# First mixture of a two-layer decoder: other queues for its loads, two scatters under way, one wait for each tile's entry

## The reference

```
x += self_attention(layernorm(x))          # layer 0, 16 heads of 64
x += cross_attention(layernorm(x), ctx)    # layer 0, 16 heads of 16
x += mixture0(layernorm(x))                # layer 0: 8 experts of 704, top 2, and a shared one of 352
x += linear_attention(layernorm(x))        # layer 1
x += cross_attention(layernorm(x), ctx)    # layer 1, 16 heads of 64
x += mixture1(layernorm(x))                # layer 1: 64 experts of 128, top 8, and a shared one
```

## Time and profile before

| | us |
|---|---|
| median of 3 runs | 3784.36 |
| lowest, highest | 3773.11, 3792.74 |
| the profiled execution, whole | 3764.9 |
| its span (first to last instruction) | 3763.2 |
| TensorE busy | 3304.6 (88%) |
| VectorE, ScalarE, GpSimd busy | 1865.9, 1650.9, 846.2 |

### The profile page before, as it was taken

The page is one execution under the profiler, slowest core; times in us unless marked ns, Lnnn a source line. Parts: engine busy times, 40 slices in busy tenths (PEclk is TensorE's granted clock), DMA queues, the critical chain, the costliest instruction groups (busy, mean ns, idle before and its releaser), DMA issues. The chain is left out here.

```text
span 3763.2 us, 76649 instructions
## 1 busy us (share of the span) xinstructions
PE 3304.6 (88%) x24490; PEld 2470.7 (66%) x24491; DVE 1865.9 (50%) x5115; ACT 1650.9 (44%) x4558; POOL 846.2 (22%) x920
## 2 busy tenths in 40 slices
PE   5999996899999777499996988999999999959882
PEld 4777775666666554277774766777777777746762
DVE  3555553677777642022221663556565665642333
ACT  2555553666666410022221325666656565621220
POOL 0000000000000033133332110132323233241774
PEclk9999998999999888799998999999999999979996
DMA  8400003000000231111112000010000000012885
GB/s 275 114 0 0 0 0 135 11 10 8 10 9 10 88 85 48 19 31 30 29 29 55 0 18 27 16 39 19 18 12 12 15 11 13 10 57 90 225 212 138
DMA packets 152369, 181.52 MB, mean 48 GB/s; under 512 B 46428, under 2 KB 126425, under 8 KB 151276
## 3 DMA queue, kind: packets, MB, share of 16 engines
q1 hardware_dynamic: 102476, 137.64, 12.3%
q0 software_dynamic: 47808, 26.74, 4.4%
q10 hardware_dynamic: 2016, 16.25, 1.0%
HBM read 116.17 MB, written 103.88 MB: 58 GB/s over the span
## 5 line engine op out<-in xcount | busy, mean ns | idle before, releaser
L1203 DVE TENSOR_REDUCE e_nmx<-PS 128x1 f32<-128x361 f32 x416 | 221.2, 532 | 400.4 <-PE PS L1044 384.8
L1554 ACT ACTIVATE b_p<-PS,b_nmx 100x361 f32<-100x361 f32 x512 | 275.5, 569 | 162.4 <-DVE b_nmx L1641 162.4
L847 POOL DMA_INDIRECT slot_rows<-r_row,r_rows_now x256 | 255.7, 999 | 401.2 <-DVE e_p L1210 274.8
L1044 PE MATMUL PS<-e_cT,e_qT 128*128 128x361 f32 x832 | 330.1, 479 | 0.0
L1150 ACT ACTIVATE e_pT<-PS 121x384 f32<-121x384 f32 (+1 forms) x416 | 199.2, 479 | 226.2 <-PE PS L1051 219.4
L1641 DVE TENSOR_REDUCE b_nmx<-PS 100x1 f32<-100x361 f32 x512 | 247.5, 526 | 97.6 <-PE PS L1404 95.8
L2509 PE MATMUL PS<-c_wgu,c_tile_xT 128*128 x912 | 290.5, 462 | 1.3 <-ACT c_tile_xT L2564 1.3
L1051 PEld LDWEIGHTS PS<-ident,e_p 128*121 128x121 f32 x1248 | 199.7, 186 | 96.6 <-issue 1.1
L1155 ACT ACTIVATE e_p<-PS,e_nmx 128x361 f32<-128x361 f32 x416 | 232.6, 559 | 69.4 <-DVE e_nmx L1203 67.4
L2754 POOL DMA_INDIRECT sum<-f_y,f_y_token x128 | 198.8, 1553 | 124.0 <-issue 111.6
L1411 PE MATMUL PS<-ident,b_p 100*121 100x100 f32 x1536 | 221.6, 280 | 5.4 <-PEq L181 2.7
(11 more groups left out here) (325 smaller groups left out, 6477.5 us busy)
## 6 DMA issues: line engine op xcount, KB each, us to landing
f_w<-in_f_W SPq DMA_DIRECT2D x64, 384.0 KB
slot_rows<-a_empty SPq DMA_DIRECT2D x1, 21504.0 KB, 65.1
f_xg<-slot_rows SPq DMA_DIRECT2D x64, 336.0 KB
c_wgu<-in_c_GU ACTq DMA_DIRECT2D x8, 1408.0 KB, 19.0
sum<-X SPq DMA_DIRECT2D x2, 3200.0 KB, 57.2
f_sums<-sum SPq DMA_DIRECT2D x16, 400.0 KB
b_cT<-in_ctx_T SPq DMA_DIRECT2D x32, 181.5 KB, 2.3
e_cT<-in_ctx_T SPq DMA_DIRECT2D x32, 181.5 KB, 2.4
```

The costliest lines, as they stand in the source:

```text
L847: pool.indirect_dma_start(out=self.rows, in_=self.row[:, u, :], in_offset=None, out_offset=bass.IndirectOffsetOnAxis(ap=self.rows_now[:, u ...
L1044: sr.fill_done(pe.matmul(sr.at(f"s{m}", ROWS, CTX), qT[:, at:at + ROWS], cT[:, u, 0:CTX], start=True, stop=True), f"s{m}")
L1203: dve.tensor_reduce(nmx[:, m:m + 1], sr.at(f"s{m}", ROWS, CTX), AX.X, ALU.max, negate=True).then_inc(max_ready, 1)
L1554: sr.move_done(act.activation(p[:, g % 2, a, 0:CTX], sr.at(f"s{g}{a}", S, CTX), ACT.Exp, bias=nmx[:, g, a:a + 1]), f"s{g}{a}")
```

## The change

1. In cross attention, ACT waits for `b_loaded` before it starts the eight transfers of `c_wgu`.
2. In the first stage of mixture0, the loads of the shared weights and the clearing of the table go from SP's queue to ACT's. The six loads of `c_wd` (768 KB each), which ACT started at the beginning of the stage, are started at steps 5, 8, 11, 14, 17 and 20.
3. The 64 scatters use two semaphores in turn, and each waits for the one before it on its own semaphore: at most two are under way.
4. In the second stage, each tile's entry has its own wait: four semaphores in turn; SP waits for entry t - 4 before it starts entry t, GpSimd waits for an entry before it gathers with it, and VectorE before it weights y.
5. The second part of X is loaded back on ACT's queue, behind its last move; the first part stays on SP's.
6. Three semaphores named `passed` or `started` become one.

```diff
@@ tiled_cross_attention, scalar
+                act.wait_ge(loaded, 64)
+                act.wait_ge(loaded, 64)
                 for e in range(8):
                     act.dma_start(ahead_to[:, e]..., ahead_from[e]).then_inc(ahead_loaded, 16)
@@ dispatch_and_shared
+    LOAD_AT = {5: 0, 8: 1, 11: 2, 14: 3, 17: 4, 20: 5}
@@ sync
-                for t, src in ((sg, shared["G"]), (su, shared["U"]), (sd, shared["D"])):
-                    sp.dma_start(t[:], ...).then_inc(s_loaded, 16)
-                sp.wait_ge(made, 1)
-                sp.dma_start(d.table..., no_token).then_inc(table_clear, 16)
@@ gpsimd
                         for n in range(2):
+                            if b > 0:
+                                pool.wait_ge(d.sent[n], b * 16)
+                                pool.sem_inc(passed, 1)
                             pool.indirect_dma_start(
...
-                                bounds_check=d.ROOM * 128 - 1, oob_is_err=False).then_inc(d.sent, 16)
+                                bounds_check=d.ROOM * 128 - 1, oob_is_err=False).then_inc(d.sent[n], 16)
@@ scalar
-                for e in range(6):
-                    act.dma_start(d.wd[:, e]..., routed["D"][e]).then_inc(d.wd_loaded[0], 16)
+                for t, src in ((sg, shared["G"]), (su, shared["U"]), (sd, shared["D"])):
+                    act.dma_start(t[:], ...).then_inc(s_loaded, 16)
+                act.wait_ge(made, 1)
+                act.dma_start(d.table..., no_token).then_inc(table_clear, 16)
                 for n in range(STEPS):
+                    if n in LOAD_AT:
+                        e = LOAD_AT[n]
+                        act.dma_start(d.wd[:, e]..., routed["D"][e]).then_inc(d.wd_loaded[0], 16)
@@ tiled_experts, sync
-                sp.wait_ge(d.sent, d.SENT)
+                for sent in d.sent:
+                    sp.wait_ge(sent, d.SENT)
                 for t in range(T):
+                    if t >= XB:
+                        sp.wait_ge(entry_loaded[t % XB], t // XB * 16)
                     at = sp.value_load(d.place[0:1, t:t + 1], ...)
                     sp.dma_start(entry[:, t, :], ...)\
-                      .then_inc(entry_loaded[t // XB > 0], 16)
+                      .then_inc(entry_loaded[t % XB], 16)
...
-                for n, batches in enumerate((slice(0, 4), slice(4, B))):
-                    sp.dma_start(X[:, batches], x_of[:, batches]).then_inc(k.x_back[n], 16)
+                sp.dma_start(X[:, 0:4], x_of[:, 0:4]).then_inc(k.x_back[0], 16)
@@ gpsimd
-                def gather(t, v, copies):
+                def gather(t, v, copies, loads):
+                    pool.wait_ge(entry_loaded[v], loads)
+                    pool.sem_inc(started, 1)
...
-                pool.wait_ge(entry_loaded[0], XB * 16)
                 for v in range(XB):
-                    gather(v, v, v + 1)
-                pool.wait_ge(entry_loaded[1], (T - XB) * 16)
+                    gather(v, v, v + 1, 16)
@@ scalar, at its end
+                for v in range(2):
+                    act.wait_ge(added[v], (T + 1 - v) // 2 * 16)
+                act.dma_start(X[:, 4:B], ...).then_inc(k.x_back[1], 16)
@@ vector
-                def weight_y(t, v):
+                def weight_y(t, v, loads):
                     dve.wait_ge(y_free, t + 1)
+                    dve.wait_ge(entry_loaded[v % XB], loads)
+                    dve.sem_inc(started, 1)
...
-                dve.wait_ge(entry_loaded[0], XB * 16)
-                dve.wait_ge(entry_loaded[1], (T - XB) * 16)
```

More of the change, by code:

```diff
@@ L2010, in __init__ @@
         self.table = dram("table", (self.ROOM * 128, 2), I32)
-        self.sent, self.x_stored = k.sem("c_sent"), k.sem("c_x_stored")
-        self.SENT, self.UNITS = B * 2 * 16, B // 4
+        self.sent, self.x_stored = [k.sem(f"c_sent{n}") for n in range(2)], k.sem("c_x_stored")
+        self.SENT, self.UNITS = B * 16, B // 4
 def dispatch_and_shared(k, gate_src, shared, routed, d):
@@ L2245, in _ @@
             def _(act):
-                for e in range(6):
-                    act.dma_start(d.wd[:, e].rearrange("p t n -> p (t n)"), routed["D"][e]).then_inc(d.wd_loaded[0], 16)
+                for t, src in ((sg, shared["G"]), (su, shared["U"]), (sd, shared["D"])):
+                    act.dma_start(t[:], src.rearrange("(c p) n -> p c n", p=128)).then_inc(s_loaded, 16)
+                act.wait_ge(made, 1)
+                act.dma_start(d.table.rearrange("(p n) o -> p n o", p=128), no_token).then_inc(table_clear, 16)
                 for n in range(STEPS):
+                    if n in LOAD_AT:
+                        e = LOAD_AT[n]
+                        act.dma_start(d.wd[:, e].rearrange("p t n -> p (t n)"), routed["D"][e])\
+                           .then_inc(d.wd_loaded[0], 16)
                     if n < PAIRS:
@@ L2421, in tiled_experts @@
         y = sb("y", [128, 2, D])
-        entry_loaded, cleared, token_ready = [sem(f"entry_loaded{n}") for n in range(2)], sem("cleared"), sem("token_ready")
+        entry_loaded, cleared, token_ready = [sem(f"entry_loaded{v}") for v in range(XB)], sem("cleared"), sem("token_ready")
         gathered = [sem(f"gathered{v}") for v in range(XB)]
-        added, y_free, started = [sem(f"added{v}") for v in range(2)], sem("y_free"), sem("started")
+        added, y_free, started = [sem(f"added{v}") for v in range(2)], sem("y_free"), k.passed
         banks = Banks(k, 0, 6).plan(["g0", "g1", "t0", "t1", "u0", "u1"])
@@ L2457, in gather, with tile @@
                         bounds_check=B * S - 1, oob_is_err=False).then_inc(gathered[v], 16)
-                def tile(j, v, more):
+                def tile(j, v, more, loads=None):
                     pool.tensor_copy(y_token_now[:, v % 2:v % 2 + 1], entry[:, bass.ds(j, 1), 0]).then_inc(token_ready, 1)
@@ L2464, in tile @@
                         pool.sem_inc(started, 1)
-                        gather(j + XB, v, 2 * j + (XB + 2))
+                        gather(j + XB, v, 2 * j + (XB + 2), loads)
                     else:
@@ L2486, in _ @@
                     for v in range(XB):
-                        tile(XB * m + v, v, True)
+                        tile(XB * m + v, v, True, m * 16 + 32)
                         landed(pool, m * (XB // 2 * 16) + (v // 2 * 16 + 16), v)
                 for j in range((T - XB) // XB * XB, T):
-                    tile(j, j % XB, j + XB < T)
+                    tile(j, j % XB, j + XB < T, (j // XB + 2) * 16)
                     landed(pool, j // 2 * 16 + 16, j)
@@ L2591, in _ @@
                 move_h(T - 1)
+                for v in range(2):
+                    act.wait_ge(added[v], (T + 1 - v) // 2 * 16)
+                act.dma_start(X[:, 4:B], d.x_rows.rearrange("(b s) d -> s b d", s=S)[:, 4:B]).then_inc(k.x_back[1], 16)
             @block.vector
@@ L2620, in _ @@
                         multiply(j)
-                        weight_y(j - 1, v)
+                        weight_y(j - 1, v, m * 16 + 16)
                 for j in range(XB * M + 1, T):
@@ L2624, in _ @@
                     multiply(j)
-                    weight_y(j - 1, j - 1)
+                    weight_y(j - 1, j - 1, (j - 1) // XB * 16 + 16)
                 move_h(T - 1)
-                weight_y(T - 1, T - 1)
+                weight_y(T - 1, T - 1, (T - 1) // XB * 16 + 16)
         banks.done(T)
@@ L2985, in decoder @@
         k.ctx_T = ctx_T
+        k.passed = sem("wait_passed")
         k.x_back = [sem(f"x_back{n}") for n in range(2)]
```

6 lines of the change are left out of this document (2 added, 4 removed).

## The result

| | before | after |
|---|---|---|
| median of 4 runs, us | 3786.84 | 3731.69 |
| lowest, highest | 3773.11, 3792.74 | 3729.09, 3736.60 |
| ratio, 95% interval | | 0.9857 (0.9830 to 0.9884) |

The kernel after is 55 us (1.4%) faster. The forecast was 3675 with a range up to 3722; the measured time lies above it. It is close to the 3728 us of the rival "the round trip is 4.7 us".

A forecast was written before the change was run, and what follows sets the result against it. TensorE was taken to bound nearly everything, losing time to scatter stalls and late loads. Gains of 4 (cross attention), 46 (first stage), 46 (entries) and 13 (X) sum to 109 us: 3784 to 3675, range 3638 to 3722.

The forecast's parts named there:

- the round trip is 4.7 us: Rival, mixture0's first stage: 32 scatter pairs at 4.7 us end it 8 us later than before; about 3728 us, 10%.
- What bounds the stage behind the stalls: Mixture0's first stage: GpSimd's 32 scatter pairs at 3.0 us each end it at 1459 instead of 1505.3, gaining 46 us.
- The stalls go: Mixture0's first stage: two scatters under way remove the late releases, worth 45 us on TensorE's side.
- the full queue: Mixture0's first stage: GpSimd's full queue of pending indirect DMAs, about 12, holds up other engines' semaphore traffic.
- The rival that the stalls stay with two under way: Mixture0's first stage: scatter traffic itself delays releases, so only 6 us are gained there; 3715 us, 17%.
- Layer 1's pairs disturb nobody: Layer 1's scatters, few pending, cause no stalls: evidence that a full queue, not scatters as such, does; no size given.
- The stage's start: Start of mixture0's first stage: putting off six `c_wd` transfers lets the first `c_xn` store land sooner; 6 us.
- Cross attention's start: Cross attention: waiting before the eight `c_wgu` transfers lets weights and contexts land sooner; gain 4 us, bounds −3 and 9.
- The entries: Mixture0's second stage: a wait per tile's entry removes TensorE's stop before the first down product; 46 us, bounds 41 and 48.
- the slower rival: Second stage's tile loop: added waits make GpSimd the bound, up to 3835 us; 4%.
- X on two queues: Start of linear attention: SP issues eight small loads without being stuck behind X's big transfer; 13 us, bounds 0 and 18.
- The rival that nothing comes of it: Linear attention's start: X and weights share DMA engines, so the other queue gains 0; 3688 us, 12%.

The follow-up runs named there:

- e10: The kernel after, but each scatter waits for the one before it (one under way): 3832 us in one run, before 3786 on that chip.
- e5: The kernel before, unchanged, traced on a chip where before takes 3717 us: 3716 us, ratio 1.000.
- e1: The kernel after with the scatters' wait taken away (free scatters): 3639 us against 3717 for before, ratio 0.979.
- e12: The kernel after with scatters in groups of two, 3 to 4 under way: 3686 us against 3787 for before, ratio 0.974.
- e9: The kernel before with only the limit of two scatters under way: 3802 us against 3786 for before, ratio 1.004.
- e16: The kernel before with only the ACT wait before `c_wgu` and X back on two queues: 3756 us against 3778, ratio 0.994.
- e8: The kernel before with only the per-tile entry waits; scatters alternate between two semaphores and wait for none: 3666 us against 3717, ratio 0.986.
- e7: The kernel before with only shared weights and clearing on ACT's queue and `c_wd` spread: 3710 us against 3717, ratio 0.998.
- e6: The kernel after, unchanged (two scatters under way), on a chip where before takes 3717 us: 3716 us, ratio 1.000.
- e11: The kernel after with free scatters again, on a chip where before takes 3786 us: 3717 us, ratio 0.982.

## Why the prediction was wrong

By its steps, as they stood, against the traces of before and after:

- **What bounds the stage behind the stalls: right place, wrong price.** The prediction named GpSimd as late next and took 3.0 us for a pair of scatters, from packets that had ended 1.8 us after a scatter's start. The trace has 4.90 and e10 4.12 for a scatter alone, of which 3.0 in the median pass up to its landing: the semaphore came well behind the 1.8 us of the last packet seen. Its upper bound, 4.7 from the landing of the additions, was the nearer row after all, although a scatter moves 800 bytes and an addition 128 KB: 32 × 4.90 = 157 us instead of 96. The first scatter started 5.5 us sooner than the 1361 taken, so the first entry load is issued at 1517.38 instead of the 1461 that a stage end of 1459 implies. This one term is 56 us; the miss by the medians is 3731.7 − 3675 = 57. The step that failed is this price of a pair.
- **The stalls go: right.** TensorE reached its last down product 62.1 us sooner; the forecast had 4 + 6 + 45 = 55. The reason given for them, the full queue, does not hold: it is not enough (e5 and e1, full queue and no stalls, on chips of the other kind) and it is not needed (e12, stalls at four). What stays is that they come from scatters under way together, that they grow with their number or rate, and that they show on some chips only. The rival that the stalls stay with two under way fell.
- **"Layer 1's pairs disturb nobody": wrong, in the trace of before.** The window of rows 7 holds additions to `sum`, not layer 1's scatters of token rows (line 847). At the end of layer 1's cross attention those run back to back, without waiting for earlier ones, and late releases stand in two of the bursts (12 scatters from 3294.52, 16 from 3373.54), though in none of the third between them:

```profile
3294.52 1.04 POOL L847 DMA_INDIRECT slot_rows<-r_row,r_rows_now  x1 [0.21 <-issue]
...
3305.89 0.53 DVE L1203 TENSOR_REDUCE e_nmx<-PS 128x1 f32<-128x361 f32 x1 [9.32 <-remote]
...
3396.22 0.90 ACT L2834 ACTIVATE f_s_gated<-PS 128x400 f32<-128x400 f32 x2 [10.69 <-remote]
```

  Together they are 39 us in 7 waits in before, 44 in after and 38 to 50 in each trace of e9 to e16, whatever the depth in mixture0; in e1 to e8 there are none in the whole trace. So the change left this part of the stalls untouched.
- **The stage's start:** 6 us forecast, 5.0 measured in the first pair of traces (the first scatter starts 11.4 us sooner, 6.5 of them from cross attention), and e7 confirms the direction with 7.6 us for the part alone.
- **Cross attention's start:** 4 forecast; ScalarE's first move came 8.1 sooner, mixture0 6.5. The eight issues took 3.97 us, started behind the wait for the weights, instead of the 7.54 that the sum carried over from the earlier trace rows.
- **The entries:** 46 forecast, 43.1 measured (e8: 46.8 in its trace for the part alone). The first down product had no stop before it. GpSimd's slack per tile was not used up, 104.6 us of waiting for y in 54 tiles, and a tile takes what it took, (1993.49 − 1538.46) / 56 = 8.1 us, so the slower rival had no ground.
- **X on two queues:** 13 forecast, 10.2 measured (TensorE's wait is 24.28 us instead of 34.51); `d_wq` was issued in 0.40 us and all eight by 2008.2, sooner than forecast, but the last weight released TensorE 13 us after its own issue at 2007.67, where the sum had 7. The rival that nothing comes of it falls with this and with e16.

Up to linear attention the sum of the measured terms is −6.5 − 5.0 − 50.7 + 68.8 − 43.1 − 10.2 = −46.7 us, where 68.8 is what the scatters took back behind the last down product (1523.41 − 1516.76, and the 62.1 that had been gained). The forecast had −109. Of the 62 between them 59 are the first stage (from its first product to the first tile's 13 slower, instead of 46 faster), and the other terms are within 3 each. The medians give 55 and not 47; where the other 8 come from no trace shows, and that the rival "the round trip is 4.7 us" lands 4 us from the measured time is partly luck, though its step is the right one. The chance of 10% for the round trip was too low for a price whose only direct row was a landing of 3.8 us.

## What to carry to other kernels

A wait on an earlier DMA of the same kind costs at least its whole round trip divided by the number under way; here a scatter took 4.12 us with one, 2.45 with two and 1.90 with three under way, where 4.12 divided gives 2.06 and 1.37. Price it from a row of landing plus release, and not from packets or from the rate of issuing. Before a limit on what is under way, count: 64 scatters at that price against the work beside them. When a stall is to be removed, run the kernel before on several chips first, and look for the same wait in the whole trace; here the stall was worth 51 us on one kind and nothing on the other, and the cure cost 64 to 69 us on both.

## What the runs showed of the hardware that was not expected

- The same kernel before differs by 1.6 to 1.9% between chips (3717 against 3778 to 3787 us). Of the 55 us between the traces of before and e5, 46 arise by the end of mixture0's first stage, where the late releases stand (the same down product at 1453.07 against 1498.86), and 12 between the starts of two bursts of layer 1's scatters, which have late releases too (3249.30 and 3316.10 against 3294.52 and 3373.54).
- An indirect DMA of 100 rows of 8 bytes takes 4.12 us from its start to the start of one that waits for it; two under way take 4.8 to 4.9 a pair (e9, e6, after), three in turn (1476.9 − 1357.3) / 63 = 1.90 each.
- Where "remote" is named, VectorE took up the logits of a `choose` 10 us late (e11, `c_logit`). What in the chip delays the release, and why only on some chips, stays open; no run parted the number under way from the rate, which free scatters spaced out in time, or few of them issued at 1.3 us, could do.
